# Two idle products of TensorE ahead of the leaf products and ahead of the first values

## The reference

```python
mem = DECAY * mem + sdt
hard = (mem > THR)
alpha = sigmoid(abt + alpha_spike * spike)
s = s * alpha[..., None]
u = einsum('bhd,bhdv->bhv', kt, s)
s = s - beta[..., None] * einsum('bhd,bhv->bhdv', kt, u)
s = s + beta[..., None] * einsum('bhd,bhv->bhdv', kt, vt)
out = einsum('bhdv,bhd->bhv', s, qt)
```

## Time and profile before

| what | value |
|---|---|
| runs before | 1795.77, 1800.31, 1802.99 us; median 1800.31 us |
| the profiled execution | 1800.0 us, span 1798.0 us, mean granted clock of TensorE 0.863 |
| TensorE busy | 80% of the span |
| VectorE busy | 71% of the span |
| ScalarE, GpSimd busy | 35%, 20% |

### The profile page before, as it was taken

The page is one execution under the profiler, slowest core; times in us unless marked ns, Lnnn a source line. Parts: engine busy times, 40 slices in busy tenths (PEclk is TensorE's granted clock), DMA queues, the critical chain, the costliest instruction groups (busy, mean ns, idle before and its releaser), DMA issues. The chain is left out here.

```text
span 1798.0 us, 47051 instructions
## 1 busy us (share of the span) xinstructions
PE 1439.5 (80%) x18540; PEld 951.3 (53%) x18568; DVE 1280.8 (71%) x3341; ACT 631.8 (35%) x1342; POOL 351.8 (20%) x515
## 2 busy tenths in 40 slices
PE   2587989797978887797879897897879887964785
PEld 0352765365626653475536663575437654742765
DVE  5578577966887758866887678775896678535564
ACT  4331354124522353133522352234413441222664
POOL 1210131014200330014101420024001410111232
PEclk8568997899699978898889978897889879986998
DMA  8991001000010001000100001000100010021223
GB/s 246 310 294 31 8 8 32 12 14 21 9 24 22 5 21 31 19 8 20 31 1 22 23 9 24 22 5 20 31 18 15 13 26 16 10 77 63 72 68 126
DMA packets 128140, 81.99 MB, mean 46 GB/s; under 512 B 75185, under 2 KB 118513, under 8 KB 127922
## 3 DMA queue, kind: packets, MB, share of 16 engines
q1 hardware_dynamic: 124466, 69.94, 14.4%
q0 software_dynamic: 3456, 8.95, 1.6%
HBM read 27.72 MB, written 51.15 MB: 44 GB/s over the span
## 5 line engine op out<-in xcount | busy, mean ns | idle before, releaser
L790 POOL COPY kx<-kend_t 32x256 f32<-32x256 f32 x256 | 103.1, 403 | 776.2 <-PE ps L1367 755.5
L1302 PE MATMUL ps<-wv,ident 128*128 128x512 f32 x320 | 175.3, 681 | 10.1 <-DVEq L1681 10.1
L1758 DVE SCALAR_TENSOR_TENSOR state<-state,gam,ps 128x128 f32<-128x128 f32 x512 | 137.4, 340 | 41.4 <-PE ps L1367 36.5
L1700 DVE TENSOR_TENSOR nv<-ps,nrm 128x512 f32<-128x512 f32 x64 | 44.3, 691 | 135.2 <-PE ps L1219 134.9
L1367 PE MATMUL ps<-w,kx 128*64 128x128 f32 x2048 | 125.9, 276 | 0.0
L1302 PEld LDWEIGHTS ps<-wv,ident 128*128 128x128 f32 x320 | 68.2, 223 | 98.8 <-issue 81.0
L1670 DVE TENSOR_TENSOR nv<-kq,kq_blk 128x31 f32<-128x31 f32 (+15 forms) x248 | 114.7, 462 | 7.4 <-DVE kq L1663 1.4
L1367 PEld LDWEIGHTS ps<-w,kx 128*64 128x64 f32 x2048 | 110.5, 137 | 12.7 <-issue 12.7
L233 PE MATMUL ps<-eleaf,wf 128*128 128x512 f32 x112 | 69.4, 753 | 46.4 <-DVEq L1681 27.1
L1545 DVE TENSOR_TENSOR kq_leaf<-kq,eleaf 128x1024 f32<-128x1024 f32 x32 | 42.2, 1319 | 89.8 <-ACT kq L886 89.6
L1006 ACT ACTIVATE w<-ps 128x512 f32<-128x512 f32 x64 | 38.2, 597 | 167.2 <-PE ps L1323 167.2
(11 more groups left out here) (313 smaller groups left out, 3339.4 us busy)
## 6 DMA issues: line engine op xcount, KB each, us to landing
slot_d<-row SPq DMA_DIRECT2D x16, 2064.0 KB, 21.3
xin<-slot_d SPq DMA_DIRECT2D x39, 129.0 KB, 2.1
a_d<-yt SPq DMA_DIRECT2D x8, 512.0 KB, 2.6
kq_blk<-a_d SPq DMA_DIRECT2D x32, 128.0 KB, 2.8
u_d<-kq SPq DMA_DIRECT2D x8, 512.0 KB, 2.6
ub<-u_d SPq DMA_DIRECT2D x128, 32.0 KB, 1.9
wall<-in_w SPq DMA_DIRECT2D x8, 512.0 KB, 7.7
xt<-in_xT POOLq DMA_DIRECT2D x8, 256.0 KB, 3.4
```

The costliest lines, as they stand in the source:

```text
L790: m = pool.tensor_copy(kx[part, :, b4, :], kend_t[part, g, 2 * q:2 * q + 2, :])
L1302: pe.matmul(bw.t[:, :], ident[:, :], wv[:, 0:512], start=True, stop=True)
L1758: k = dve.scalar_tensor_tensor(out=state[:, hp, b, :], in0=state[:, hp, b, :], scalar=gam[:, hp, b:b + 1], in1=bd[j].t[:, DV * x:DV * x + ...
```

## The change

A new function issues n products of the identity with 512 columns of `wv` into bank `bv`, each with start and stop set, so that the next real product overwrites them. It waits first until the bank is free for this chunk's first values, and increments no bank semaphore. It is called with n = 2 ahead of leaves(1), leaves(2) and leaves(3), and ahead of values(c, 0), in each of the eight chunks.

```diff
+        def hold_clock(c, n):
+
+            pe.wait_ge(bv.drained.sem, bv.freed(c, "v0"))
+            settle(c)
+            for k in range(n):
+                pe.matmul(bv.t[:, :], ident[:, :], wv[:, 0:512], start=True, stop=True)
+
...
             for p in range(1, HP):
+                hold_clock(c, 2)
                 leaves(c, p, runs)
                 if p + 1 < HP:
                     keys(c, p + 1)
...
+            hold_clock(c, 2)
             values(c, 0)
             if nxt:
                 pe.wait_ge(bn.drained.sem, bn.emptied(c, "ss"))
```

## The result

The changed kernel takes 1815.28 us (median of 6 runs, 1810.44 to 1818.06); the kernel before, on the same chip, 1801.65 us (6 runs). The ratio is 1.0067, with a 95% interval of 1.0039 to 1.0096: slower by 12 us, between 7 and 17. The ratio and its interval are taken over all the runs and are not the quotient of the two medians; wherever this text gives what a version costs or gains in us, it is the ratio less one, times the time of the kernel before. The forecast was 1819 us, slower by 19, in a range of 1798 to 1838.

A forecast was written before the change was run, and what follows sets the result against it. VectorE was taken to bound the pairs stage (94% busy), with TensorE nearly as full. Terms of 4, 9.5 and 15.5 us made 29, less 10 for a lifted clock: +19 on 1800.0, so 1819 us, range 1798 to 1838.

The forecast's parts named there:

- The root of the forecast: In the pairs, TensorE is late, not idle, where the products go in, and VectorE has no room either.
- The price: TensorE time of each call's four matmul instructions: 1.9 us at the upper clock level, 3.7 at the lower.
- Call 1, 4 us: Products ahead of leaves(1): keys(2) come 1.9 us later, partly given back; 4 us over eight chunks, bounds -10 to 15.
- The term that was taken off it: At keys(2), later leaf_products(2) overlap GpSimd's difference less, ending 0.9 us later instead of 1.9 in the third chunk.
- Call 2, 9.5 us: Products ahead of leaves(2), 3.7 us in the third chunk, delaying keys(3): 9.5 us over eight chunks, bounds 0 to 30.
- Calls 3 and 4, 15.5 us: Products ahead of leaves(3) and values: gate late, y1 waits at the solve's start; 15.5 us in all, bounds 0 to 32.
- The rebate of 10 us: Products ahead of leaves(1) and leaves(3) partly lift the clock for squares, turn_ends and mean_square: 8 x 1.3, 10 us off.
- Rival (a): Products ahead of leaves(1) keep the clock up to keys(3) and pay for the rest: no change, about 1804 us; chance 0.22.
- Rival (b): Clock pays more than it costs: the long waits for keys(2) in four chunks vanish, 1790 us; chance 0.08.
- Rival (c): All four calls run at the lower level and raise nothing in time: 14.8 us of TensorE per chunk, 1848; chance 0.10.
- Rival (d): The change does not do what it says; 128 added instructions in the profile would refute it; no chance stated.

The follow-up runs named there:

- The waits alone: The changed kernel with both loops of added products emptied and its four waits per chunk kept, against the kernel before: 1799.06 us against 1799.02, ratio 0.9994.
- the other order: Kernel before with keys(1) issued and copied out ahead of the last chunk's turned tiles, no products added: ratio 0.9923, on another chip 0.9964.

## Why the prediction was right or wrong

The time came out 12 us slower where 19 were forecast, inside the stated range. The root of the forecast holds in part. TensorE is late rather than idle at these places, and a product there does push back what stands behind it. But it does not follow that each product goes on top: of 80.8 us that the products take, 29.8 remain in TensorE's busy time and 12 in the kernel's. By its steps:

*The price.* 1.8 us per call at the upper level, against 1.9 forecast, and 3.6 at the lower, against 3.7. The four calls took 77.8 us in all from their starts to the next instruction, 2.4 on average; 128 instructions at the upper level alone would be 61 us. The 80.8 us of the profile count the overlap of consecutive instructions too.

*Call 1, 4 us.* Measured alone 1 us, with an interval of -3 to +6. The term that was taken off it, for the instructions beside GpSimd's difference, was the right one and somewhat undersized: 1.7 us of 1.9 came back in the third chunk, where the forecast was 1.0. None of the four slow leaf_products(2) of the kernel before (1.7 to 2.0 us) is left in the changed kernel.

*Call 2, 9.5 us.* Measured alone 6, between 1 and 12. The step that came out otherwise is the level: the call was put at 3.7 us, and it took 2.0 in the third chunk and 1.8 to 2.8 in five of the eight. It is not call 1 that did this: alone, with no call 1 ahead of it, call 2 took 1.8 to 3.1 us. In three chunks it ran at the lower level or nearly (3.4 to 3.6 us from its start to leaves(2)); in two of them VectorE then waits 0.7 us for keys(3), in the last 5.31.

*Calls 3 and 4, 15.5 us.* Measured alone 4 and 0, with intervals of -1 to +9 and -4 to +4. In the sum for the third chunk, 1.7 us stand for call 3 without a row that gives them; the call took 2.8 us there and its leaves gained nothing (2.23 us). Otherwise the mechanism is in the trace as told, to the 1.8 us at y1 in five chunks of eight, and the solves' 12.8 us more are near the sum. But the wait was priced as if nothing gave it back, and that is wrong: call 4 alone makes the same wait and costs nothing. The first chunk's front end and the last reload of the rows return more than half of it in that profile, and the forecast, which followed the path forward to y1 only, did not look for what else moves when y1 is late.

*The rebate of 10 us* was the guess of the prediction, and its reason did not come: of squares, turn_ends and mean_square, which call 1 was to lift, turn_ends(1) ran at the lower level in seven chunks of eight and mean_square in six of its seven. What the clock did give lies elsewhere. The keys of pair 2 ran at the upper level throughout in eight chunks, where it was four, and leaves(2) in seven, where it was none. The clock from 20 to 50 us into a chunk rose from 0.69 to 0.82, and over the span from 0.863 to 0.887, a little more than the one or two hundredths expected. The four calls measured alone add up to 11 us with no rebate at all, so the runs give it no size of its own.

So the total is near by luck in part, through errors of opposite sign: the entry of the solve was charged 15.5 us and cost about 4, calls 1 and 2 were charged 13.5 and cost about 7, and 10 us were taken off for a lift that did not happen as told. The forecast also said that the solves would be as long as before, which cannot stand beside waits at y1, since y1 is in the solve.

*Rival (a)*, no change because call 1 holds the clock up, did not come: its signs were turn_ends(1) at the upper level and no wait at y1, and neither is there. Call 4 is free alone although y1 waits, so not for this reason. Call 1 alone had turn_ends(1) at the upper level in four chunks of eight; for it the rival is half true. That four dense key instructions are each time followed by a rise, as the prediction has it, is not so each time: behind keys(0) of the first chunk, at 62 us, the clock rises only at 88, and behind keys(2) of the seventh, at 1254, only at 1266. *Rival (b)* did not come. *Rival (c)*, products at the lower level everywhere, is out: call 1 ran at the upper level in seven chunks of eight, and calls 2 and 3 both near the lower in three. *Rival (d)* is out by the count.

The Trainium skill's figure for the clock's ramp, under 1% of a typical kernel's span (page "TensorE: Matmul & The Clock Gate", section "What's actually happening"), was turned by the prediction into a bound on all that a full clock could give, which is more than it says. No run here tests such a bound by a gain. In this kernel the lower level has 27% of the span before and 23% after, and the 82 us less of it in the front ends came with 12 us more of time.

## What to carry to other kernels

A product that is issued only to hold the clock has no price that can be read off the place where it goes in. All four calls had 0.0 us of idle time ahead of them; alone, two of them cost nothing, the other two 6 and 4 us, and one of the free ones, doubled, 41. Ask instead what waits behind the product, and what that was waiting for besides: call 4 was free while VectorE had 4.89 us of waiting for DMA to use up, and dear when 0.41 was left. Even a right forecast of a wait is no forecast of the time: follow it to the next thing that was waiting for something else, and measure one call at a time. Where an engine waits for products that stand behind less urgent ones, try the order first: here it was the only change that gained.

## What the runs showed of the hardware

Some stretches of a chunk come in a few lengths, and the chunks of one execution switch between them. From leaf_products(1) to (2) the kernel before has 9.1 us in three chunks and around 11 in three; from the solve's end to the first write, in chunks 2 to 7, it has 8.6 us in five and 11.4 in one. The second pair is the clock: the last idle products of the solve ran like this in the third and in the fourth chunk of the kernel before.

```profile
553.98 1.96 PE L1302 MATMUL ps<-wv,ident 128*128 128x512 f32 x4
750.92 3.55 PE L1302 MATMUL ps<-wv,ident 128*128 128x512 f32 x4
```

The chunk with the slow one was 4.4 us longer in its tiles (90.1 us against 85.7), behind a solve that was 1.1 us shorter. The table above counts such chunks: one in the profile before, none in the changed kernel's, four with call 3 alone. That does not show that the added products move it. The waits alone have it in two, and of the two profiles of the kernel with the other order one has it in two chunks and the other in none. So the same kernel differs in this from one execution to the next, by 4.4 us each time. That is part of why half a per cent can't be read from single profiles.

The reload of the rows' last quarter, 128 KB, took 2.8 us from issue to landing in one chunk and 4.2 in another of the same execution.

VectorE's product took 2.02 us where it overlapped GpSimd's difference and 1.23 alone, at equal size. With call 1 ahead of it, it started later and overlapped nothing, so in the third chunk the later start was nearly free.
